# A four-block transformer kernel: the third block's first keys and queries prepared in the second block, and its causal zeros and key sums on GpSimd

## What is computed

```python
x = x + tanh(g_xattn[0]) * L0_xattn(layernorm(x), ctx)   # softmax of a normalised similarity
x = x + tanh(g_ffn[0])   * L0_ffn(layernorm(x))          # 512 -> 2048 -> 512, ternary weights
x = x + tanh(g_xattn[1]) * L1_xattn(layernorm(x), ctx, ctx)
x = x + tanh(g_ffn[1])   * L1_ffn(layernorm(x))          # gated, 512 -> 2*1408 -> 512
# L1_xattn: RMS norm of q and k, rotary embedding (q * cos + rotate_half(q) * sin), 16 heads
# of 32 for q in groups of 4 to one of 4 key heads, then causal attention:
scores = where(tril, einsum('bgnqd,bgkd->bgnqk', q, k) * hd ** -0.5, -1e30)
out = softmax(scores) @ v @ w_out.T
```

## Time and profile before

| | |
|---|---|
| runs of the kernel | 956.44, 956.9, 958.63 us, median 956.9 |
| profiled execution | 959.12 us, its span 957.3 us |
| TensorE busy | 682.9 us (71%) |
| VectorE busy | 712.2 us (74%) |
| ScalarE busy | 600.7 us (63%) |
| GpSimd busy | 399.5 us (42%) |
| L1234, row maxima, VectorE | 176 instructions, 108.7 us |
| L1375, exponentials, ScalarE | 176 instructions, 94.4 us |
| L1501, mask in `shifted`, TensorE | 256 instructions, 50.4 us |
| L1115, sum of two key tiles, GpSimd | 16 instructions, 55.9 us |

### The profile page before, as it was taken

The page is one execution under the profiler, slowest core; times in us unless marked ns, Lnnn a source line. Parts: engine busy times, 40 slices in busy tenths (PEclk is TensorE's granted clock), DMA queues, the critical chain, the costliest instruction groups (busy, mean ns, idle before and its releaser), DMA issues. The chain is left out here.

```text
span 957.3 us, 14401 instructions
## 1 busy us (share of the span) xinstructions
PE 682.9 (71%) x5260; PEld 376.6 (39%) x5260; DVE 712.2 (74%) x1152; ACT 600.7 (63%) x786; POOL 399.5 (42%) x385
## 2 busy tenths in 40 slices
PE   4654026677786756056998998999999756978796
PEld 2232012333333322034565454456555323545453
DVE  3886977999999875669579379656543278989884
ACT  2547419888988892247888288559845035747575
POOL 1100542787877687727257026412212003333232
PEclk9877558979979799557998999999999978989899
DMA  8610040000000000312132111112200000000001
GB/s 332 247 32 0 0 131 1 1 1 1 1 1 1 0 1 12 115 41 92 62 112 64 31 31 62 42 62 67 67 2 2 30 0 1 24 23 33 23 30 48
DMA packets 21726, 43.68 MB, mean 46 GB/s; under 512 B 3872, under 2 KB 8480, under 8 KB 20768
## 3 DMA queue, kind: packets, MB, share of 16 engines
q1 hardware_dynamic: 21664, 42.85, 13.2%
HBM read 38.61 MB, written 4.19 MB: 45 GB/s over the span
## 5 line engine op out<-in xcount | busy, mean ns | idle before, releaser
L1234 DVE TENSOR_REDUCE c_nmax<-c_s 128x1 f32<-128x384 f32 (+3 forms) x176 | 108.7, 634 | 89.7 <-PE c_s L1471 89.7
L1375 ACT ACTIVATE c_probs<-c_e 128x512 f32<-128x512 f32 (+1 forms) x176 | 94.4, 559 | 58.5 <-PE c_e L1501 57.4
L1115 POOL TENSOR_TENSOR c_psum<-c_probs 128x1536 f32<-128x1536 f32 x16 | 55.9, 3493 | 156.8 <-ACT c_probs L1375 156.8
L1893 PE MATMUL d_gu<-gateq,d_xqT 128*128 128x352 bf16 x512 | 94.7, 336 | 13.4 <-DVE d_h L1694 12.4
L849 PE MATMUL b_y<-w2q,b_q2T 128*128 128x512 bf16 x256 | 70.2, 430 | 44.2 <-ACT b_q2T L780 21.9
L1468 PE MATMUL c_s<-c_kT,c_qaT 96*128 96x128 f16 (+3 forms) x256 | 74.3, 323 | 18.2 <-DVE c_nmax L1234 17.8
L824 PE MATMUL b_up<-w1q,b_xqT 128*128 128x512 bf16 x256 | 74.1, 417 | 2.5 <-ACT b_h L746 2.5
L1499 PE MATMUL c_e<-c_qaT,c_kT 98*128 98x512 f16 (+3 forms) x256 | 69.7, 306 | 5.3 <-ACT c_qaT L1362 4.7
L1893 PEld LDWEIGHTS d_gu<-gateq,d_xqT 128*128 128x128 bf16 x512 | 49.9, 103 | 50.0 <-DVE d_h L1694 18.4
L1822 ACT ACTIVATE d_sg<-d_gu,d_dq 128x352 f32<-128x352 f32 x64 | 35.4, 554 | 53.7 <-PE d_gu L1893 53.7
L849 PEld LDWEIGHTS b_y<-w2q,b_q2T 128*128 128x128 bf16 x256 | 25.5, 106 | 80.7 <-issue 35.6
(11 more groups left out here) (221 smaller groups left out, 1925.5 us busy)
## 6 DMA issues: line engine op xcount, KB each, us to landing
c_stage<-in_gateT SPq DMA_DIRECT2D x16, 704.0 KB, 4.1
c_stage<-in_downT SPq DMA_DIRECT2D x6, 768.0 KB, 4.4
a_wf<-in_w1T SPq DMA_DIRECT2D x2, 2048.0 KB, 13.7
a_wf<-in_w2T SPq DMA_DIRECT2D x2, 2048.0 KB, 8.5
out<-xs SPq DMA_DIRECT2D x16, 256.0 KB, 2.0
xs<-in_x SPq DMA_DIRECT2D x1, 3072.0 KB, 14.9
xs<-in_x SPq DMA_DIRECT2D x1, 1024.0 KB, 5.4
a_ctxT<-in_ctxT SPq DMA_DIRECT2D x1, 1024.0 KB, 7.4
```

Of the source, the lines that this page charges most:

```text
L1115: nc.gpsimd.tensor_tensor(psum[:], region(slot, 0)[:, :, P:], region(slot, 1), ALU.add).then_inc(psum_ready, 1)
L1234: nc.vector.tensor_reduce(nmax[:, G % 2, i, n:n + heads], s_ps[u % 2][:, 0:heads * (i + 1) * P].rearrange("p (n k) -> p n k", n=heads), ax ...
L1375: nc.scalar.activation(probs[:, G % 2, at:at + width], e_ps[fill % 3][:, 0:width], ACT.Exp).then_inc(e_read, 1)
L1893: last = nc.tensor.matmul(gu_ps[k % 2][:, half, 0:PART], xqT[:, i % 2, c, :], gateq[:, c, at:at + PART], start=(c == 0), stop=(c == CH - 1))
```

## The change

The preparation's functions move into a class, `Preparation`, whose tiles live from `ffn0` on. `kaug` and `qaug`, the split keys and queries, lie in the memory of `w1q` (now `shared`). The first batch's steps are called in `ffn0`'s rounds: keys squared at the end of p = 2; keys scaled and the statistics at the end of p = 3; all key turning, the query scale and the first query tile's turning on GpSimd in p = 4, ahead of `integers(n)`, and one more query tile in each of p = 5, 6, 7 at the same place; `weighted` behind `affine(n+1)` in p = 4, 5, 6 and once more at the end of p = 6; the splitting at the end of p = 7, after the last use of `w1q`. During `ffn0` there is a `turned` buffer for each of the four tiles.

`xattn1` starts with the first five turns, each into a bank of its own (`early_ps`), copied out by ScalarE (three) and VectorE (two). TensorE waits for the five copies and the mask before its first scores; its waits for other set-up data stand in the loop at the unit that first needs them.

In `shifted` the mask matmul is gone. GpSimd zeroes the exponentials above the diagonal instead, with one `affine_select` for each group and key tile (`causal`, 64 in all), and `weigh` and `total` wait for that. `summed` comes after the group's last unit of exponentials. The mask in the scores stays.

```diff
+class Preparation:
...
+        parts = g["shared"][:].rearrange("p c n -> p (c n)").bitcast(fp16)
+        width = TILES * HEADS * self.AUG
+        self.qaug = parts[:, 0:width].rearrange("p (t h a) -> p t h a", t=TILES, h=HEADS)
+        self.rest = parts[:, width + TILES * KV_HEADS * self.AUG:].bitcast(fp32)
+        self.kaug = parts[:, width:width + TILES * KV_HEADS * self.AUG].rearrange("p (t h a) -> p t h a", t=TILES, h=KV_HEADS)
...
+    def turned_at(self, n):
+        return self.more_turned[:, n - self.TURNED, :] if self.TURNED <= n < TILES else self.turned[:, n % self.TURNED, :]
...
+    def weighted(self, dve, b, i):
+        nc, n = self.nc, b * TILES + i
+        if n >= 1:
+            dve.wait_ge(self.xsin_ready, 2 * n)
+            dve.wait_ge(self.qcos_ready, n)
+        nc.vector.scalar_tensor_tensor(out=self.xw[:], in0=self.xs[:, n, :], scalar=self.mv[:, i, 0:1], in1=self.qw[:],
+                                       op0=ALU.subtract, op1=ALU.mult).then_inc(self.xw_ready, 1)
+        dve.wait_ge(self.xw_ready, n + 1)
+        if n >= TILES:
+            dve.wait_ge(self.qlo_ready, n - self.TURNED + 1)
+        table = self.cos[:, i, :].rearrange("p (o j) -> p o j", o=1).broadcast_to([P, HEADS, HD])
+        nc.vector.tensor_tensor(self.turned_at(n).rearrange("p (h j) -> p h j", j=HD),
+                                self.xw[:].rearrange("p (h j) -> p h j", j=HD), table, ALU.mult).then_inc(self.qcos_ready, 1)
+
...
+        shared = sb("shared", [P, CH, INNER], bf16, early)
+        prep = Preparation(nc, sb, sem, early, locals())
-        w1q = sb("w1q", [P, CH, INNER], bf16, w0)
+        w1q = shared
...
+    prep.more_turned = t("turned", [P, TILES - prep.TURNED, DIM])
...
                 sloped(n + 1)
                 second_half(n - 1)
                 affine(n + 1)
+                if 4 <= p < 7:
+                    prep.weighted(dve, 0, p - 4)
                 largest(n + 1)
                 residual(n - 1)
                 quantised(p + 2)
                 second_half(n)
+                if p == 2:
+                    dve.wait_ge(const_loaded, 112)
+                    prep.keys_squared(dve, 0)
+                if p == 3:
+                    prep.keys_scaled(dve, 0)
+                    dve.wait_ge(x_ready, TILES)
+                    for i in range(TILES):
+                        prep.statistics(dve, 0, i)
+                    prep.statistics_end(dve, 0)
+                if p == 6:
+                    prep.weighted(dve, 0, 3)
+                if p == 7:
+                    dve.wait_ge(up_done, 2 * TOTAL)
+                    prep.key_parts(dve, 0)
+                    for i in range(TILES):
+                        prep.query_parts(dve, 0, i)
 
         @block.gpsimd
         def _(pool):
...
                 inputs_scale(p + 2)
                 output_scale(n - 1)
                 output_bias(n - 2)
+                if p == 3:
+                    prep.keys_scale(pool, 0)
                 deviation(n + 1)
+                if p == 4:
+                    for i in range(TILES):
+                        prep.turn_keys(pool, 0, i)
+                    prep.keys_turned(pool, 0)
+                    prep.queries_scale(pool, 0)
+                if 4 <= p < 8:
+                    prep.turn_queries(pool, 0, p - 4)
                 integers(n)
                 integers(n + 1)
                 output_bias(n - 1)
...
                 gelu(n + 1)
                 spread(n + 1)
                 first_half(n - 1)
+                if p == 7:
+                    act.wait_ge(up_done, 2 * TOTAL)
+                    prep.keys_again(act, 0)
+                    for i in range(TILES):
+                        prep.query_heads(act, 0, i)
                 gather(n + 3)
 
         @block.tensor
...
+    early_ps = [bank[:].bitcast(fp16) for bank in (e_ps[0], e_ps[1], e_ps[2], y_ps, av_ps)]
+    EARLY_BY = ("act", "dve", "act", "dve", "act")
...
-                pool.wait_ge(e_read, exp_of(G, 7))
+                pool.wait_ge(causal_done, G * TILES + 2)
                 if G:
                     pool.wait_ge(den_done, G)
                 nc.gpsimd.tensor_tensor(psum[:], region(slot, 0)[:, :, P:], region(slot, 1), ALU.add).then_inc(psum_ready, 1)
 
+            def causal(G, k):
+                pool.wait_ge(e_read, exp_of(G, (3, 7, 9, 10)[k]))
+                part = region(G % 2, k)[:, :, 0:P]
+                nc.gpsimd.affine_select(part, part, [[0, GROUP], [1, P]], ALU.is_ge, 0.0, 0, -1).then_inc(causal_done, 1)
+
...
-                G, r = group(u - LAG - 7)
+                for k, at in ((0, 3), (1, 7), (2, 9), (3, 10)):
+                    G, r = group(u - LAG - at)
+                    if r == 0 and 0 <= G < GROUPS:
+                        causal(G, k)
+                G, r = group(u - LAG - PER)
                 if r == 0 and 0 <= G < GROUPS:
                     summed(G)
...
+            def early_out(k):
+                b, what = TURNS[k]
+                dve.wait_ge(early_done, k + 1)
+                nc.vector.tensor_copy(turned_to(what, b), heads_of(early_ps[k])).then_inc(early_read, 1)
...
-            dve.wait_ge(const_loaded, 112)
-            keys_squared(0)
-            for i in range(TILES):
-                statistics(0, i)
-            statistics_end(0)
-            keys_scaled(0)
             nc.vector.tensor_copy(mask[:], maskf[:]).then_inc(setup, 1)
...
+            choices()
+            for k in range(EARLY):
+                if EARLY_BY[k] == "dve":
+                    early_out(k)
...
-                take("tr", tr_read, k + 1)
+                if k < EARLY:
+                    bank, done = early_ps[k], early_done
+                else:
+                    bank, done = tr_ps[:], tr_done
+                    take("tr", tr_read, later(k))
...
-                    nc.tensor.matmul(e_ps[fill % 3][:, m * width:(m + 1) * width], kT[0:FULL, b % 2, grp, k * P:(k + 1) * P],
-                                     qaT[0:FULL, h + m, k * P:], start=True, stop=False)
-                    last = nc.tensor.matmul(e_ps[fill % 3][:, m * width:m * width + P], mask[:], ident_b[:],
-                                            start=False, stop=True)
+                    last = nc.tensor.matmul(e_ps[fill % 3][:, m * width:(m + 1) * width], kT[0:FULL, b % 2, grp, k * P:(k + 1) * P],
+                                     qaT[0:FULL, h + m, k * P:], start=True, stop=True)
...
-                pe.wait_ge(e_read, exp_of(G, (3, 7, 9, 10)[k]))
+                pe.wait_ge(causal_done, G * TILES + k + 1)
...
-                pe.wait_ge(e_read, exp_of(G, PER - 1))
+                pe.wait_ge(causal_done, (G + 1) * TILES)
...
-            pe.wait_ge(const_loaded, 112)
             for k in range(EARLY):
                 turn(k)
-            pe.wait_ge(setup, 6)
-            pe.wait_ge(psetup, 5)
-            pe.wait_ge(wo_loaded, 16)
+            pe.wait_ge(early_read, EARLY)
+            pe.wait_ge(setup, 1)
             for u in range(END):
                 if u < UNITS:
                     scores(u)
+                if u == LAG:
+                    pe.wait_ge(setup, 2)
+                if u == TOTALLED:
+                    pe.wait_ge(psetup, 5)
+                if u == EXPANDED:
+                    pe.wait_ge(setup, 6)
+                if u == PROJECTED:
+                    pe.wait_ge(wo_loaded, 16)
                 if 0 <= u - LAG < UNITS:
                     shifted(u - LAG)
                 for k in range(2):
```

More of the change, by code:

```diff
@@ L1182, in statistics @@
-            def statistics(b, i):
-                small.mark(nc.vector.bn_stats(bn[:, i, :], xs[:, b * TILES + i, :]))
-            def statistics_end(b):
-                dve.wait_ge(step, small.value())
-                for i in range(TILES):
-                    last = small.mark(nc.vector.bn_aggr(mv[:, i, :], bn[:, i, :]))
-                dve.wait_ge(step, last)
-                nc.vector.tensor_scalar(vq[:], mv[:, :, 1], HD * (1.0 + EPS), HD * EPS * EPS, ALU.mult, ALU.add).then_inc(vq_ready, 1)
@@ L1230, in maximum, with choices @@
+            def choices():
+                for i in range(TILES):
+                    nc.vector.tensor_copy(chosen[:, i, :].rearrange("p (n d) -> p n d", d=HD),
+                                          ident[:].rearrange("p (n c) -> p n c", c=HD)[:, :, i:i + 1].broadcast_to([P, GROUP, HD])
+                                          ).then_inc(setup, 1)
             def maximum(u):
@@ L1416, in _ @@
                     if TURN_AT[k] == u:
[L1417 removed]
+                        turned_out(k)
                 b = u // SPAN + 1
```

341 lines of the change are left out of this document (169 added, 172 removed).

## The result

| | before | after |
|---|---|---|
| runs of the kernel | median 957.45 us (956.44 to 959.66, 8 runs) | median 963.69 us (960.58 to 966.6, 8 runs) |
| profiled execution, span | 959.12, 957.3 us | 960.58, 958.6 us |
| TensorE's mean granted clock | 0.875 | 0.868 |
| attention: first maximum to the last exponential's end | 418.6 to 738.3, 319.7 us | 404.3 to 734.4, 330.1 us |
| from there to VectorE's first instruction of the last block | 23.2 us | 28.1 us |

The ratio is 1.0059, 95% interval 1.0042 to 1.0076: slower by 6 us, where 9 us less was forecast. So the traces show what the loop and its end lose and what the move gains, but some 4.8 of the 6.2 us between the medians are in neither.

The account below looks back on a forecast made before the run. VectorE was taken to bound the feed-forward stage and TensorE the attention, with a 37.0 us prologue between. Terms: -30.4 + 23.6 - 11 + 5 + 3.9 = -8.9 us, giving 948.0 us, range 932 to 963.

Parts of the forecast that it names:

- Prologue: 37.0 to 6.6: Attention's start: five transposes into separate banks bring the first scores after 6.6 us instead of 37.0, gaining 30.4 us.
- The feed-forward stage: +23.6: First feed-forward stage: the moved preparation lengthens it by 23.6 us, summed over tile pairs p=2 to p=7, bounds 14 and 32.
- 256 mask matmuls ... three quarters: -11 us: Attention: dropping 256 mask matmuls of 0.058 us saves 14.8, three quarters counted, so -11 us; bounds 0 and -14.8.
- The wait hides ... +5 us, bounds 0 and 12: Attention: waits for GpSimd's 0.9 us selects hide in the steady part; where queries are turned, selects and sum add 5 us.
- The end of the block: Attention's end: `total` waits for the last select and the sum of key tiles, +3.9 us with nothing covering it.
- Terms at bounds together give 933 to 968: Whole kernel: span of the result with terms at their bounds, widened to a range of 932 to 963 us.
- A: Rival: feed-forward gaps hold the moved work, the stage grows only 14 us and selects hide; 933.4 us, chance 0.22.
- B: Rival: GpSimd's selects in attention are dear, 3.46 us each, making the kernel slower; 968 us, chance 0.16.
- C: Rival: moved work costs in the feed-forward stage what it cost before, growth 32 us; 956.4 us, chance 0.12.
- What would show it: Trace signs: attention starts near 404, scores 6 to 7 us later, `affine(11)` 13 us later, selects near 0.9 us.

Follow-up runs that it names:

- P alone: Changed kernel with mask matmuls restored, no selects and the early sum, leaving only the moved preparation: 943.6 us (0.9844 of before), 945.0 us in a second set.

## Why the prediction was wrong

**Prologue: 37.0 to 6.6.** Right, 5.0 us measured. The copy behind the last transposes took the 1.1 forecast. The five turns took 3.7 us from 398.81 and not 5 x 1.09: 1.09 is the duration of a record, and from start to start a turn's eight matmuls take less, 24 of them 2.55 us at clock 0.50 and the next eight, from 401.36 to 401.90, 0.54 us while the clock rises.

**The feed-forward stage: +23.6.** Right in kind, a little too much. The same `affine` of tile 4, ahead of every edit, stands 1.8 us earlier in after, so the growth is 18.2 + 1.8 = 20.0 us at the stage's end:

```profile
212.51 2.34 DVE L607 SCALAR_TENSOR_TENSOR b_h<-b_h,b_rstd,b_ln_b 128x2048 f32<-128x2048 f32 x1
```

```profile
210.71 2.34 DVE L773 SCALAR_TENSOR_TENSOR b_h<-b_h,b_rstd,b_ln_b 128x2048 f32<-128x2048 f32 x1
```

By pairs, from the starts of `affine` of tiles 8, 10, 12, 14 and of `residual(14)` (3.5, 9.3, 10.6, 15.0 and 18.2 us later than in before, each plus the 1.8), forecast and measured: p=2 and 3, 6.0 and 5.3; p=4, 7.4 and 5.8; p=5, 1.0 and 1.3; p=6, 2.8 and 4.4; p=7, 6.4 and 3.2. The rows of p=4, as the earlier trace rows:

```profile
281.68 2.50 DVE L773 SCALAR_TENSOR_TENSOR b_h<-b_h,b_rstd,b_ln_b 128x2048 f32<-128x2048 f32 x1
...
292.90 2.35 DVE L734 TENSOR_SCALAR b_xq<-b_xc 128x1024 bf16<-128x1024 f32 x1
...
295.17 1.85 DVE L736 TENSOR_SCALAR b_dq<-b_d,w_scale 128x2 f32<-128x2 f32 x1
...
302.62 0.69 DVE L794 COPY b_q2T<-b_t 128x1024 bf16<-128x1024 bf16 x1
...
282.00 3.09 POOL L171 TENSOR_TENSOR c_xsin<-c_xk,ssin 128x64 f32<-128x64 f32 x2
...
292.58 2.13 POOL L883 TENSOR_SCALAR b_h<-b_h,b_qs 128x2048 f32<-128x2048 f32 x1
...
294.79 2.21 POOL L888 TENSOR_SCALAR b_q<-b_h 128x2048 bf16<-128x2048 f32 x1
```

Against the start of their pair, which is itself 3.5 us late, the integers start 10.7 us late (forecast 13.2), and `second_half(8)` 5.8 (4.5). What I had not seen: VectorE's steps of `quantised` fall beside the late integers and are stretched (1024 values for each partition 2.35 us instead of 0.69, and two values 1.85 instead of 0.22), while the odd `affine` is freed, 2.50 instead of 4.00. And of the end, as the earlier trace rows:

```profile
365.84 0.75 DVE L802 SCALAR_TENSOR_TENSOR xs<-b_y,b_dq,xs 128x512 f32<-128x512 f32 x1 [1.17 <-POOL b_dq L877]
...
384.87 0.69 DVE L794 COPY b_q2T<-b_t 128x1024 bf16<-128x1024 bf16 x1 [4.47 <-PE b_t L1037]
...
385.47 1.62 DVE L183 CAST shared<-c_ksq 128x512 f16<-128x512 f32 x1
...
391.49 0.75 DVE L802 SCALAR_TENSOR_TENSOR xs<-b_y,b_dq,xs 128x512 f32<-128x512 f32 x1
...
372.11 5.50 POOL L229 TENSOR_TENSOR c_xsin<-c_xw,ssin 128x256 f32<-128x256 f32 x2
```

`key_parts` and the query parts take 5.9 us where 8.4 were forecast, and `residual(14)` follows at once: its idle time of 5.41 in the earlier trace rows has covered nearly all of them. The waits for the integers come ahead of them (4.47). The last tile's first turning step, 1.92 in the earlier trace rows, takes 5.50 beside VectorE's two steps of 2.35 us over the hidden values.

Together the move gives -12.0 in the trace (-6.8 forecast), and 12.8 to 14.9 in the medians of P alone. This half of the forecast was right in sign and low by some 5 to 8.

**"256 mask matmuls ... three quarters: -11 us".** Mis-sized: -5.9. The 0.058 us each hold where TensorE sets the pace, and that is the part from unit 116 on, a third of the units, not three quarters; and in the stretches where VectorE sets it, TensorE's clock fell a little further (0.60 instead of 0.75).

**"The wait hides ... +5 us, bounds 0 and 12".** This is the step that failed. The select's price was near, 0.68 us for my 0.9. But selects alone cost 9.8 us (8.5 net of the masks), and the late sum 11.6 to 15.6. The end of the block, that I had at +3.9, grew by 4.9 to 5.0: 2.7 by the later `total` and 2.2 behind it, at the lower clock; of the late sum's price it is 2 to 3. In medians, one part after another, the move gave -14.9 (-6.8 forecast) and the missing masks -5.9 (-11), and then the selects took +14.4 (952.1 - 937.7) and the late sum +11.6, together 26 us where I had 5 + 3.9. I put the sum's collision only where queries are turned. I did not look for what stands in VectorE's list at the sum's new units, 4 and 15 of each batch: at 5 there is `keys_scaled`, at 16 `weighted`. The rule that I had cited, the Trainium skill, SBUF — State Buffer, section Who interferes with whom, has the price: a VectorE instruction with two SBUF inputs and a GpSimd one that reads SBUF exclude each other. By that rule, the trace agrees: 1.13 + 3.58 is 4.71 us, and 4.69 was measured. I applied it to the feed-forward stage and not to the loop.

And I took slack from the program's units (weigh three to eight units behind), not from the queue: a select stands behind the sum and the turning, and is late by their length. The sum of the term has a slip too: it counts 0.9 for each batch where the sentence ahead of it has two tiles' selects, 1.8.

**The range.** "Terms at bounds together give 933 to 968" is not what the terms give: -30.4 + 14 - 14.8 + 0 + 3.9 is 930, and -30.4 + 32 - 0 + 12 + 3.9 is 974. The 933 and 968 are rivals A and B. The range was too narrow at its upper end by my own bounds, and 963.7 lies inside them.

**Rivals.** A, the gaps hold the work, holds in part in the feed-forward stage: p=7 did hide its parts, and 20.0 measured lies between its 14 and my 23.6, nearer mine. B, slower by late selects (968 us from 2.0 us a select), had the right side and the right place, but not the lever: at 0.68 us the queue ahead of the select decides. C was wrong: the stage grew by 20.0 us and not by 32.

**What would show it.** Scores 5.0 us behind the block's start (6 to 7 forecast), selects 0.68 (0.9), TensorE's idle time before the last `total` 2.5 (3.5): near. The block starts at 398.65, between A's 394 and my 404. `affine` of tile 11 comes 9.3 us later than in before, 11.1 with the 1.8 (13). VectorE does not wait ahead of `second_half(8)`, and a query part takes 0.7 us, not 1.5 or more. From the first scores to the last exponential 6 us less than 320.8: it is 330.8, 10 more. TensorE's masks were not hidden by ScalarE, as I had feared, but by VectorE.

## What to carry to other kernels

When a long GpSimd instruction moves, list what VectorE does in the units where it lands: a 3.5 us instruction holds up every two-input VectorE step that it meets for what is left of its length, and in this pipeline the loss grew to about twice the stretching, and two units of distance gave back some 10 us. Work moved to an engine that is only half busy isn't free if it stands in that engine's queue behind long instructions and something waits for it. Try the parts of a change one by one: here one part was worth 13 to 15 us and the other two cost 20.

## What the runs showed of the hardware

`affine_select` on GpSimd, float32 and in place, takes 0.63 us over 128x4x128 and 0.29 over 128x128 where nothing disturbs it, so its time falls by less than its size. A GpSimd add of 3.46 to 3.58 us that reads SBUF held up a short VectorE step with two SBUF inputs for nearly its whole length (1.13 us became 4.69). Without 256 matmuls TensorE's granted clock was lower in a stretch where TensorE wasn't the limit (0.60 from 423 to 440 us, against 0.70 to 0.80 in seven traces that keep them there), and 1.00 as before where it was.
